# Output projection and first dense layer of a fused attention and MoE block: multiplied into one weight, and its stage dropped

## The chip, the cores and the metric

The kernel runs on 1 core of one Trainium2 chip. The metric is device time in microseconds (us) of one execution. A core has engines with queues of their own: TensorE (PE; its weight loads are listed as PEld), VectorE (DVE), ScalarE (ACT), GpSimd (POOL), and SyncE (SP), which issues the DMAs. They wait for one another by semaphores. TensorE multiplies a stationary 128x128 tile with a moving tile of up to 512 columns into one of eight PSUM banks.

## The reference

All in fp32, for x of 2 batches x 1024 tokens x 256 features:

```
q, k, v = x @ Wq.T + bq, ...            # 16 heads of 16
a   = sparse_attention(q, k, v)         # each query attends to 32 listed keys (or a dense form, by u_prev)
o   = a @ Wo.T + bo                     # output projection, 256 -> 256
h   = relu(o @ w1 + b1)                 # first dense layer, 256 -> 1024
x1  = x + h @ w2 + b2                   # 1024 -> 256
g   = gelu(x1 @ fc1.T + f1b)            # 256 -> 1024
c   = concat(g @ fc2.T + fc2_b, g @ experts[index].T + experts_b[index])   # 1024 -> 192 + 64
out = x1 + top-2-of-8 gated experts of c (router, 8 products 256 -> 256)
```

There is nothing between the projection and the first dense layer, so that h = relu(a @ (Wo.T @ w1) + (bo @ w1 + b1)).

## The kernel before

**Two paths.** The data decide at run time between a path for few distinct keys (`Few`, at most 256 of them; this is the one that runs with these inputs) and one for all keys (`Attention`). Both end in the same dense stage.

**Attention (Few).** An opening spreads the index lists, counts keys, and projects q, k, v on TensorE. Then `due()` lists the work in order of a time t, and each engine's function walks this one list and emits its own part. There are 64 "guard" jobs (8 units of 8), one at each t: TensorE forms guard scores of 128 queries against 256 keys for four heads, in two PSUM banks (lines 504 and 506; a job may only begin when VectorE has taken the maxima of the job two before it), and VectorE takes the maxima (line 737). 12 steps later (`LAG`) comes "score" job n = t - 12: TensorE, 2 products of 512 queries (line 524), ScalarE's exponential into `Pr` (line 657), VectorE's weighing (line 744). In between stand query transposes ("query_rows", line 489, copied by ScalarE at 649), key transposes ("score_keys", "guard_keys"), values products (line 540), and per unit "take", "norm" and "turn", which bring the result into `attT`. The banks of `psM` are handed out in turn over one list, `misc_order`: a user waits until the last but one has been copied out. `attention_done` is set by the copy of the last turn.

**Exact products.** Products of the dense stage are made of tiles rounded to a faster fp32 form (fp32r), each split into a rounded part hi (ScalarE or VectorE cast) and a rest lo (VectorE or GpSimd subtraction): `mm3` issues lo x hi, hi x lo, hi x hi, three products of 128x512 (lines 1544 to 1546). A plain fp32 product instead is run by the chip as two instructions.

**Weights.** `pieces` lists the weights in pieces of 128x1024 (fp32): early Wo (half a piece), w1 in two, w2 in two; late fc1 in two, WcA, WcB0, WcB1 (second layer of the second block), ew in four. SP loads piece i into slot i % 2 of `staged`, once the piece two before it is split (`load_pieces`, lines 1459 to 1472); ScalarE casts hi (`split_hi`, line 1478), GpSimd or VectorE subtracts lo (`split_lo`, line 1484). Early pieces are split during attention: ScalarE at guard jobs 4, 12, 20, 28 and 36, GpSimd at 6, 14, 22, 30 and 38. Late pieces are split in dense jobs named by `LATE_AT`; those with an even index by GpSimd, with an odd one by VectorE.

**Dense stage.** Four chunks of 512 tokens (`CHUNKS`). `dense_jobs` writes the order of jobs out: for a chunk, "h" (8 jobs of 6 products), "y" (2 jobs of 24), "gelu" (8 of 6), "c" (2 of 24), and for the chunk before, "router" and "experts" between them. The output projection is stage "ao", 2 jobs of 6 products per chunk: chunk 0's first of all, chunk 1's one before gelu 0 of chunk 0 and one behind gelu 7, those of chunks 2 and 3 between gelu and c of the chunk before. Its input is the attention output split in two (`attention_hi` on ScalarE, `attention_lo` on GpSimd, into tile `cT`), and its output `aoT` is evacuated by ScalarE (+ bias) into one of three buffers `V` and split by VectorE. All engines walk the jobs in this order. `AHEAD_AT` puts the first four jobs (ao 0, ao 1, h 0, h 1) between the last steps of attention on TensorE and ScalarE; of these, VectorE splits the two ao jobs ahead too, since the tile of h lies over memory that attention still uses.

**For the change** note: the first 12 guard jobs run with no score work beside them; `Pr` holds the exponentials from score 0 on and is free at tiles 2 to 5 before; `cols` holds the bias columns (bo 2, b1 8, b2 2, f1b 8).

## Time and profile before

| | |
|---|---|
| median of 3 runs | 569.64 us (569.31 to 569.93) |
| profiled execution | 570.82 us |
| its span in the trace | 568.4 us |
| TensorE busy | 521.5 us (92%) |
| VectorE busy | 408.6 us (72%) |
| ScalarE busy | 225.7 us (40%) |
| GpSimd busy | 84.2 us (15%) |

The trace is of one execution, some 2.4 us shorter than that execution's own time, since the span runs from the first to the last recorded instruction. Matmuls are pipelined: an instruction's listed time overlaps that of the next, so their cost in a row is the distance of their starts. "Granted clock" is the share of TensorE's full 2.4 GHz; 0.50 is 1.2 GHz. The opening runs to 56.41 us, guard jobs alone to 78.11, attention to about 271.3, and the dense stage to the end.

### The profile page before, as it was taken

To read this page: it belongs to the slowest core of one execution; us is meant where nothing else is said; L and a number is where in the kernel's file an instruction comes from. 1 tells how busy PE (TensorE), PEld (TensorE's weight loads), DVE (VectorE), ACT (ScalarE), POOL (GpSimd) and SP (SyncE) were. 2 spreads that over 40 slices of the span, in tenths; PEclk is the share of its full clock that TensorE was granted. 3 is DMA by queue.
4 is the path that set the end of the run, shared out by engine and by line. 5 is a ranking of instruction groups with operands and counts; after the bars stand their busy time and mean duration, and the time that the engine had idled before them with its cause. 6 is when DMAs were issued, how large, how long until landed. Compare 5 with 4: busy or idle time off the path is not lost.

```text
span 568.4 us, 7403 instructions
## 1 busy us (share of the span) xinstructions
PE 521.5 (92%) x2649; PEld 360.3 (63%) x2649; DVE 408.6 (72%) x788; ACT 225.7 (40%) x381; POOL 84.2 (15%) x94
## 2 busy tenths in 40 slices
PE   3897888999899999889969999999999999999896
PEld 1454445454454445436748887888878888788775
DVE  4887879878887777845867598483884839847295
ACT  4204476667665656764526240042400415003100
POOL 3002544315133120300141000010000100000000
PEclk9999699999999999999999999999999999999999
DMA  7200011101010000000451000100001000010000
GB/s 250 57 2 0 1 37 38 37 2 38 1 39 1 1 0 2 1 1 0 114 146 38 1 1 20 46 10 0 2 18 47 11 2 0 20 46 2 9 12 31
DMA packets 11756, 15.37 MB, mean 27 GB/s; under 512 B 5954, under 2 KB 8258, under 8 KB 11714
## 3 DMA queue, kind: packets, MB, share of 16 engines
q1 hardware_dynamic: 11714, 14.83, 8.5%
q8 instruction: 24, 0.39, 0.3%
q14 instruction: 18, 0.15, 0.1%
HBM read 12.73 MB, written 2.10 MB: 26 GB/s over the span
## 4 chain that ended last, share of the span: by engine, by line
PE 39%; DVE 6%; POOL 2%; issue 1%; DMA 1%; ACT 1%; SPq 0%; DVEq 0%; POOLq 0%
PE psG L1546 4%; PE psG L1545 4%; PE psG L1544 4%; PE psM L1544 3%; PE psM L1545 3%; PE psM L1546 3%; PE psS L1544 3%; PE psS L1545 3%; PE psS L1546 3%; PE psO L1544 3%; PE psO L1546 3%; PE psO L1545 3%; DVE hT_lo L1694 1%; DVE hT_hi L1692 1%; DMA staged<-ew_dram 1%
## 5 line engine op out<-in xcount | busy, mean ns | idle before, releaser
L737 DVE TENSOR_REDUCE few_Qa<-psG 128x2 fp32r<-128x512 f32 x116 | 74.7, 686 | 28.5 <-PE psG L506 28.4
L657 ACT ACTIVATE Pr<-psS 128x512 f32<-128x512 f32 x128 | 71.4, 599 | 28.5 <-PE psS L528 19.5
L744 DVE SCALAR_TENSOR_TENSOR Pr<-Pr,few_W 128x1024 f32<-128x1024 f32 x48 | 72.8, 1520 | 10.2 <-ACT Pr L657 10.1
L524 PE MATMUL psS<-few_QAT,few_KP 128*128 128x512 f32 x128 | 52.9, 457 | 10.5 <-ACT Pr L657 9.8
L504 PE MATMUL psG<-few_KG,QG 128*128 128x512 f32 x116 | 53.0, 515 | 2.9 <-DVE few_Qa L737 2.9
L1655 ACT ACTIVATE V<-psS,cols 128x512 f32<-128x512 f32 x16 | 11.0, 690 | 103.3 <-PE psS L1546 102.6
L1694 DVE TENSOR_TENSOR hT_lo<-V,hT_hi 128x512 fp32r<-128x512 f32 x64 | 46.5, 726 | 2.2
L506 PE MATMUL psG<-Mneg,few_identb 128*128 128x512 bf16 x116 | 46.8, 403 | 0.0
L524 PEld LDWEIGHTS psS<-few_QAT,few_KP 128*128 128x128 f32 x128 | 22.3, 188 | 38.2 <-issue 30.7
L1692 DVE CAST hT_hi<-V 128x512 fp32r<-128x512 f32 x64 | 34.2, 535 | 12.7 <-ACT V L1655 6.2
L540 PE MATMUL psO<-Pr,few_VA 128*17 128x512 f32 x256 | 33.5, 598 | 0.0
L1668 POOL TENSOR_TENSOR cT_lo<-attT,cT_hi 128x1024 fp32r<-128x1024 f32 x4 | 9.6, 2391 | 143.8 <-ACT cT_hi L1631 143.8
L706 DVE TENSOR_SCALAR few_EQ<-few_idxb,cst 128x1024 f16<-128x1024 f16 x64 | 28.8, 504 | 2.5 <-ACT few_idxb L588 2.5
L506 PEld LDWEIGHTS psG<-Mneg,few_identb 128*128 128x128 bf16 x116 | 11.4, 98 | 30.0 <-issue 29.8
L649 ACT CAST few_QAT<-psM 128x512 fp32r<-128x512 f32 x32 | 18.9, 590 | 21.0 <-PE psM L489 21.0
L504 PEld LDWEIGHTS psG<-few_KG,QG 128*128 128x128 f32 x116 | 23.4, 201 | 5.7 <-issue 4.2
L1692 DVE CAST cT_hi<-V 128x512 fp32r<-128x512 f32 x8 | 3.4, 427 | 32.7 <-ACT V L1660 32.7
L1544 PE MATMUL psO<-ew_lo,cT_hi 128*128 128x512 f32 x64 | 26.2, 410 | 0.4 <-DVE y L1806 0.4
L1544 PE MATMUL psM<-ew_lo,cT_hi 128*128 128x512 f32 x64 | 26.0, 406 | 0.2 <-DVE y L1806 0.2
L1546 PE MATMUL psO<-ew_hi,cT_hi 128*128 128x512 f32 x64 | 25.5, 398 | 0.0
L1545 PE MATMUL psO<-ew_hi,cT_lo 128*128 128x512 f32 x64 | 25.4, 397 | 0.0
L1545 PE MATMUL psM<-ew_hi,cT_lo 128*128 128x512 f32 x64 | 25.1, 392 | 0.0
(251 smaller groups left out, 1194.7 us busy)
## 6 DMA issues: line engine op xcount, KB each, us to landing
Pr<-xT_dram SPq DMA_DIRECT2D x2, 1024.0 KB, 8.6
staged<-w_dram SPq DMA_DIRECT2D x4, 512.0 KB, 3.7
x1T<-xT_dram SPq DMA_DIRECT2D x4, 512.0 KB, 4.2
staged<-ew_dram SPq DMA_DIRECT2D x4, 512.0 KB, 4.0
out_dram<-y SPq DMA_DIRECT2D x16, 128.0 KB, 1.7
staged<-fc_dram SPq DMA_DIRECT2D x2, 512.0 KB, 3.8
Pr<-wqkv_dram SPq DMA_DIRECT2D x1, 768.0 KB, 4.9
staged<-fc2a_dram SPq DMA_DIRECT2D x1, 512.0 KB, 3.4
```

What stands on the lines that cost most here:

```text
L504: nc.tensor.matmul(o, QG[:, (u // 2) % 2, st * P:st * P + P], self.KG[:, u % 2, 2 * p:2 * p + 2, :], start=True, stop=False)
L506: mm = nc.tensor.matmul(o, self.identb[:, :], Mneg[:, None, st * FEW_KEYS:(st + 1) * FEW_KEYS].to_broadcast([P, 2, FEW_KEYS]), start=False ...
L524: mm = nc.tensor.matmul(psS[:, f, :], self.KP[:, u % 2, j, r * P:r * P + P], self.QAT[:, u % 2, j // 2, q], start=True, stop=not logged)
L540: mm = nc.tensor.matmul(psO[VW * j:VW * j + VC, part, :], self.VA[:, b, r, h * VC:h * VC + VC], Pr[:, HG * r + j, 512 * part:512 * part + ...
L657: nc.scalar.activation(Pr[:, i % JOBS, 512 * f:512 * f + 512], psS[:, f, :], ACT.Exp, scale=SCALE).then_inc(self.s["s_exp"], 1)
L737: nc.vector.tensor_reduce(self.Qa[:, f % SLOTS, st, 2 * p:2 * p + 2, 48], self.guard_bank(i)[0][:, p, :].rearrange("p (h t) -> p h t", h=2 ...
L744: nc.vector.scalar_tensor_tensor(pr, pr, FMAX, self.W[:, r, :], ALU.min, ALU.mult).then_inc(self.s["s_prob"], 1)
L1544: nc.tensor.matmul(ps, w[0], a[1], start=start, stop=False)
L1545: nc.tensor.matmul(ps, w[1], a[0], start=False, stop=False)
L1546: return nc.tensor.matmul(ps, w[0], a[0], start=False, stop=stop)
L1692: link(nc.vector.tensor_copy(tile.hi[at], v))
L1694: nc.vector.tensor_tensor(tile.lo[at], v, tile.hi[at].bitcast(F32), ALU.subtract).then_inc(d["parts"], 1)
```

## The change

The two weights are multiplied once, Wo.T @ w1, on TensorE in plain fp32, and the joint bias b1 + bo @ w1 too. `Wo` and `w1` are loaded whole (w1 into both slots of `staged`), five "fuse" steps are listed at t = 0, 1, 3, 5 and 7 of `due()`, each behind the guard job of that t on TensorE: steps 0 to 3 make a quarter of the product each, step 4 the bias. ScalarE copies a quarter to `Pr` (tiles 2 to 5) and casts it to `w1.hi`; GpSimd makes `w1.lo`. ScalarE's first exponential waits for the four quarters. The stage "ao" is gone from the jobs, h reads the split attention output (now tile `aT`, one buffer for all chunks, refilled behind the chunk's last h job), and the jobs ahead of `attention_done` are h 0, h 1, h 2. Early pieces are now the two halves of w2, loaded behind step 4 and split in the places where w1's halves were (guard jobs 12/14 and 20/22). Late pieces have indices lower by three, so the engine that makes their lo changes.

```diff
+FUSED = 5
-AHEAD_AT = (1, 1, 4, 6)
+AHEAD_AT = (1, 2, 4)
+FUSED_AT = (0, 1, 3, 5, 7)
@@ due(), behind guard and the other entries of t
+                    for j in range(FUSED):
+                        if t == FUSED_AT[j]:
+                            yield "fuse", j
@@ misc_order()
+                    if what == "fuse":
+                        order.append(("fuse_out", i))
@@ Few.pool
-                    if what == "guard" and i % JOBS == 6 and i // JOBS < len(EARLY):
-                        split_lo(nc.gpsimd, pool, EARLY[i // JOBS:i // JOBS + 1])
+                    if what == "guard" and i % JOBS == 6 and 1 <= i // JOBS <= len(EARLY):
+                        split_lo(nc.gpsimd, pool, EARLY[i // JOBS - 1:i // JOBS])
+                    if what == "fuse" and i < FUSED - 1:
+                        fuse_lo(pool, i)
@@ Few.tensor
+                    if what == "fuse":
+                        fuse_tensor(pe, i, misc("fuse_out", i))
@@ Few.act
+                    if what == "fuse":
+                        fuse_act(act, i, self.misc_bank("fuse_out", i))
...
                     if what == "score":
                         if i == 0:
                             act.wait_ge(self.s["log_lo"], 1)
+                            act.wait_ge(d["fused"], FUSED - 1)
@@ pieces
-        early.append(("Wo", flat(Wo, 0, 512), [("WoT", 0, 512)]))
-        for name, w in (("w1", w1), ("w2", w2)):
-            for h in range(2):
-                early.append((name, flat(w, h * 1024, 1024), [(name, h * 1024, 1024)]))
+        for h in range(2):
+            early.append(("w2", flat(w2, h * 1024, 1024), [("w2", h * 1024, 1024)]))
@@ load_pieces
-                if i >= 2:
+                if i < 2:
+                    sp.wait_ge(d["fuse_full"], FUSED)
+                else:
                     sp.wait_ge(LD[f"w_lo{i % 2}"], i // 2)
@@ new
+        def load_fused(sp):
+            sp.dma_start(Wo[:, :, :], io["Wo"]).then_inc(LD["ld_wo"], 16)
+            sp.dma_start(staged[:, :, :], io["w1"]).then_inc(LD["ld_w1"], 16)
+        def fuse_tensor(pe, i, ps):
+            if i == 0:
+                pe.wait_ge(LD["ld_wo"], 16)
+                pe.wait_ge(LD["ld_w1"], 16)
+            if i < FUSED - 1:
+                rows_, _, cols_ = fused_part(i)
+                for o in range(KD):
+                    mm = nc.tensor.matmul(ps, Wo[:, o, rows_], staged[:, o, cols_], start=(o == 0), stop=(o == KD - 1))
+            else:
+                pe.wait_ge(L["cols"], 16)
+                nc.tensor.matmul(ps[:, 0:KW], ident, b1_in, start=True, stop=False)
+                for k in range(KW):
+                    for o in range(KD):
+                        mm = nc.tensor.matmul(ps[:, k:k + 1], staged[:, o, k * P:k * P + P], bo[:, o:o + 1],
+                                              start=False, stop=(k == KW - 1 and o == KD - 1))
+            mm.then_inc(d["fuse_full"], 1)
+        def fuse_act(act, i, ps):
+            act.wait_ge(d["fuse_full"], i + 1)
+            if i < FUSED - 1:
+                whole = Pr[:, 2 + i, 0:512]
+                nc.scalar.copy(whole, ps).then_inc(d["fuse_out"], 1)
+                act.wait_ge(d["fuse_out"], i + 1)
+                nc.scalar.copy(w1.hi[fused_part(i)[1]], whole).then_inc(d["fuse_hi"], 1)
+            else:
+                nc.scalar.copy(b1[:, :], ps[:, 0:KW]).then_inc(d["fuse_out"], 1)
+        def fuse_lo(pool, i):
+            pool.wait_ge(d["fuse_hi"], i + 1)
+            w = fused_part(i)[1]
+            nc.gpsimd.tensor_tensor(w1.lo[w], Pr[:, 2 + i, 0:512], w1.hi[w].bitcast(F32), ALU.subtract).then_inc(d["fused"], 1)
@@ dense_jobs
-            yield from jobs_of("ao", 0, range(KD), "act")
...
-                if c == 0:
-                    yield from jobs_of("ao", 1, range(1), "act")
...
-                    if c + 1 < CHUNKS:
-                        yield from jobs_of("ao", c + 1, range(c == 0, KD), "act")
@@ dense_tensor
-                if stage == "ao":
-                    weights("Wo")
+                if stage == "h":
+                    if n == 0:
+                        pe.wait_ge(d["fused"], FUSED - 1)
                     pe.wait_ge(d["at_lo"], c + 1)
...
-        LATE_AT = (("h", 2), ("h", 3), ("h", 5), ("h", 6), ("y", 0), ("y", 0), ("gelu", 1), ("gelu", 4), ("c", 0))
+        LATE_AT = (("h", 3), ("h", 4), ("h", 5), ("h", 6), ("y", 0), ("y", 0), ("gelu", 1), ("gelu", 4), ("c", 0))
@@ attention_hi
-            if c >= 2:
-                act.wait_ge(d["v_full"], number["experts", c - 2, TT * 5 - 1] + 1)
-            nc.scalar.copy(cT.hi[:, :, :], attT[:, :, c * QC:(c + 1) * QC]).then_inc(d["at_hi"], 1)
+            if c:
+                act.wait_ge(d["a_full"], number["h", c - 1, KW - 1] + 1)
+            nc.scalar.copy(aT.hi[:, :, :], attT[:, :, c * QC:(c + 1) * QC]).then_inc(d["at_hi"], 1)
@@ dense_vector
-                    if stage == "ao":
-                        if c and i == 0:
-                            dve.wait_ge(d["a_full"], number["h", c - 1, KW - 1] + 1)
-                        split(aoT, v, at)
```

## Rows read from the trace of the kernel before

**Rows 1.** The page's chain of work that ended last, shares by engine.

```profile
PE 39%; DVE 6%; POOL 2%; issue 1%; DMA 1%; ACT 1%; SPq 0%; DVEq 0%; POOLq 0%
```

**Rows 2.** Busy us (x instructions) by stretch: PE, PEld, DVE, ACT, POOL; clock, DMA, GB/s.

```profile
60.00:64.00 4.00, 2.43 (x6) 1.00 (x5) 4.00 (x6) 2.88 (x4) 0.90 (x1) 0.50 0.00 0
68.00:72.00 4.00, 3.96 (x21) 2.16 (x19) 3.40 (x7) 1.78 (x4) 4.00 (x9) 0.99 0.00 0
...
360.00:380.00 20.00, 20.00 (x90) 16.53 (x90) 14.05 (x24) 5.25 (x8) 2.43 (x1) 1.00 0.02 7
```

**Rows 3.** Timeline, TensorE, first guard job to first score: start us, us, instruction.

```profile
56.41 0.77 PE L504 MATMUL psG<-few_KG,QG 128*128 128x512 f32 x1
...
68.39 0.58 PE L504 MATMUL psS<-few_KG,QG 128*128 128x512 f32 x1
...
69.32 0.58 PE L504 MATMUL psG<-few_KG,QG 128*128 128x512 f32 x1
...
69.97 0.60 PE L489 MATMUL psM<-cst,few_Qa 128*128 128x128 f32 x4
70.33 0.47 PE L504 MATMUL psS<-few_KG,QG 128*128 128x512 f32 x1
...
76.64 1.04 PE L572 MATMUL psM<-cst,Qn 128*128 128x128 f32 x8
...
78.11 0.71 PE L524 MATMUL psS<-few_QAT,few_KP 128*128 128x512 f32 x2
```

**Rows 4.** Timeline, VectorE: the first guard job's maxima.

```profile
61.01 1.28 DVE L737 TENSOR_REDUCE few_Qa<-psG 128x2 fp32r<-128x512 f32 x2
```

**Rows 5.** Timeline, TensorE: plain fp32 products of the projections.

```profile
45.92 1.89 PE L432 MATMUL psM<-Pr 128*128 128x256 f32 x8
```

**Rows 6.** Router products after a gap (timeline), and two stretches with their clock.

```profile
537.20 0.25 PE L1606 MATMUL psM<-rw,cT_hi 128*128 128x16 f32 x1 [2.06 <-DVE cT_lo L1694]
537.30 0.25 PE L1607 MATMUL psM<-rw,cT_lo 128*128 128x8 f32 x1
...
284.00:288.00 4.00, 0.91 (x4) 0.43 (x4) 3.00 (x4) 1.82 (x3) 2.34 (x1) 1.00 0.64 139
...
539.20:543.20 4.00, 4.00 (x13) 3.20 (x12) 3.55 (x29) 0.23 (x1) 0.00 (x0) 0.58 0.01 2
```

**Rows 7.** Timeline: guard jobs 24, 40 and 56; a weight split and VectorE beside it.

```profile
113.23 0.40 PE L504 MATMUL psG<-few_KG,QG 128*128 128x512 f32 x1
...
163.66 0.39 PE L504 MATMUL psG<-few_KG,QG 128*128 128x512 f32 x1
...
213.04 0.40 PE L504 MATMUL psG<-few_KG,QG 128*128 128x512 f32 x1
...
133.00 2.38 POOL L1484 TENSOR_TENSOR w_lo<-staged,w_hi 128x1024 fp32r<-128x1024 f32 x1
...
133.29 3.18 DVE L744 SCALAR_TENSOR_TENSOR Pr<-Pr,few_W 128x1024 f32<-128x1024 f32 x1
```

**Rows 8.** Timeline, TensorE: the last turn of attention.

```profile
269.47 1.03 PE L561 MATMUL psM<-cst,few_An 128*128 128x128 f32 x8
```

**Rows 9.** Timeline, hand-over to the dense stage: GpSimd, ScalarE, VectorE, TensorE.

```profile
276.42 2.39 POOL L1484 TENSOR_TENSOR fc_lo<-staged,fc_hi 128x1024 fp32r<-128x1024 f32 x1 [43.56 <-ACT fc_hi L1478]
...
283.27 1.05 ACT L1478 CAST WcB_hi<-staged 128x1024 fp32r<-128x1024 f32 x1 [2.00 <-DMA staged<-experts_dram]
...
296.89 0.69 DVE L1694 TENSOR_TENSOR x_lo<-x1T,x_hi 128x512 fp32r<-128x512 f32 x1
...
296.72 0.68 PE L1544 MATMUL psS<-cT_lo,Wo_hi 128*128 128x512 f32 x1 [2.51 <-POOL cT_lo L1668]
...
299.33 0.63 PE L1544 MATMUL psS<-x_lo,fc_hi 128*128 128x512 f32 x1
```

**Rows 10.** Timeline, TensorE, chunk 1: first product of ao, first of c.

```profile
380.89 0.39 PE L1544 MATMUL psS<-cT_lo,Wo_hi 128*128 128x512 f32 x1
...
383.61 0.39 PE L1544 MATMUL psG<-hT_lo,WcA_hi 128*128 128x512 f32 x1
```

More of the change, by code:

```diff
@@ L400, in misc @@
                     if n >= 2:
-                        pe.wait_ge(self.s[order[n - 2][0]], order[n - 2][1] + 1)
+                        before, k = order[n - 2]
+                        pe.wait_ge((d if before == "fuse_out" else self.s)[before], k + 1)
                     return self.misc_bank(name, i)
@@ L724, in vector @@
                 for what, i in self.due():
-                    if what == "ahead" and i < KD:
-                        if i == 0:
-                            dve.wait_ge(self.s["q_lo"], FILLS)
-                        dense_vector(dve, jobs[i:i + 1], i)
                     if what == "guard":
@@ L1537, in bass_adaln_ffn @@
         for stage, c, i, e, n in jobs:
-            if stage in ("ao", "h", "y", "gelu", "c"):
+            if stage in ("h", "y", "gelu", "c"):
                 split_no[stage, c, i] = len(split_no) + 1
@@ L1569, in dense_tensor @@
                 cols_ = slice(i * P, i * P + P)
[L1570 to L1571 removed]
+                if stage == "h":
+                    if n == 0:
+                        pe.wait_ge(d["fused"], FUSED - 1)
                     pe.wait_ge(d["at_lo"], c + 1)
                     for k in range(KD):
[L1574 to L1579 removed]
+                        mm = mm3(ps, parts(w1, ALL, k, cols_), parts(aT, ALL, k, ALL), k == 0, k == KD - 1)
                 if stage == "y":
@@ L1834, in loads @@
                 if not att.dense:
+                    load_fused(sp)
                     load_pieces(sp, EARLY, eid)
@@ L1874, in work @@
                     attention_lo(pool, 0)
+                    for i in range(FUSED - 1):
+                        fuse_lo(pool, i)
                     split_lo(nc.gpsimd, pool, EARLY)
@@ L1886, in work @@
                 if att.dense:
+                    for i in range(FUSED):
+                        if i >= 2:
+                            pe.wait_ge(d["fuse_out"], i - 1)
+                        fuse_tensor(pe, i, psM[:, i % 2, :])
                     dense_tensor(pe, jobs[0:len(AHEAD_AT)])
@@ L1899, in work @@
                     attention_hi(act, 0)
+                    for i in range(FUSED):
+                        fuse_act(act, i, psM[:, i % 2, :])
                     split_hi(act, EARLY)
@@ L1913, in work @@
                 dve.wait_ge(s["attention_done"], 1)
-                if att.dense:
-                    for i in range(KD):
-                        dense_vector(dve, jobs[i:i + 1], i)
                 dve.wait_ge(L["cols"], 16)
-                dense_vector(dve, jobs[KD:], KD)
+                dense_vector(dve, jobs, 0)
             either(dve, work)
```

43 lines of the change are left out of this document (20 added, 23 removed).

## Prediction

> **What bounds the kernel now.** I read the page's chain of waits first: of the work that ended last, TensorE holds by far the largest share, VectorE the next [rows 1]. Since shares average stages with different limits, I went on to busy time by stretch. In the dense stage TensorE is busy 20.00 of 20 us [rows 2], at 2.4 GHz: each product taken out is worth its own spacing. In the opening, 60 to 64 us, it is busy 2.43 of 4 us at a granted clock of 0.50 (1.2 GHz), while VectorE is busy throughout; from 68 us on the clock is back and TensorE is busy 3.96 of 4 [rows 2]. Third came the timelines of the three stretches that the change touches: the opening from the first guard job (56.41) to the first score (78.11) [rows 3], the attention tail [rows 8], and the hand-over to the dense stage, where weights pass through a two-slot staging buffer [rows 9].
>
> **Dense products removed.** In steady chunks the two "ao" jobs of the next chunk (12 products) stand between 380.89 and the first product of "c" at 383.61: 2.72 us with no gap [rows 10]. Chunks 2 and 3 give 2 x 2.72 = 5.44 us. Chunk 1's second job (6 products) is worth half: 1.36. What would be late next is "c" waiting for VectorE's last gelu split, but that comes eight weight tiles into "c", 7 x 0.68 = 4.8 us after it starts, and one evacuation and one split are under 2 us: hidden. If VectorE had more backlog than that, it would cost the excess. Sum: -6.8.
>
> **Attention tail.** Twelve products (ao 0) between last score and values become h0 and h1, the same twelve; h1 no longer stands between norm and the last turn, and h0's wait on VectorE's ao split goes. The turn began at 269.47 [rows 8], while its input was ready about 0.3 us earlier: -0.5 at most, and it reaches only the start of the hand-over, so I book it there.
>
> **Hand-over.** Before, the first gelu product is at 299.33: ao 1's first job waited 2.51 us for the attention split, and ran with the start of gelu 0 at the low clock, 0.43 apart, not 0.23 [rows 9]. I do not book this wait as won, because something else is late: VectorE's last x1 split ended at 297.58 [rows 9]. The early weight pieces fall from five to two, so the parity of every late piece flips: fc1's first half, WcA and WcB1 go to GpSimd (2.39 each [rows 9]; VectorE takes half of that), and the first half of ew goes to VectorE, in front of y0's evacuation. A GpSimd split also stretches whatever VectorE starts beside it: 1.2 us became 3.18 [rows 7]. One leg of the staging chain is split, refill and landing: GpSimd's fc split ended at 278.81, the next tile was cast from 283.27, 4.46 us [rows 9]. ScalarE casts in job order, so each leg delays the evacuation queued behind it. Walking the chain from an attention end 0.5 earlier: WcA landed at about 280.4, WcB0 284.3, h7's split done 287.6 (as before), WcB1 288.3, ew0 290.5, its split on VectorE until 292.7, y0 and y1 evacuated and split by 297.4. So gelu 0 starts 1.9 us earlier, having stood idle longer; it starts at the low clock, and I charge 1.9 for that against 0.5 paid before. Together with the tail: -0.4. Bounds: if the clock holds and no split is stretched, -3; if each GpSimd split delays VectorE in full once more, +2.
>
> **Weight splits removed from the attention stage.** w1's and w2's four halves are cast and split in guard jobs 12/14, 20/22, 28/30 and 36/38; after, only two remain, in the first two places. Sixteen guard jobs with two splits took 113.23 to 163.66, 50.43 us; the next sixteen, without, 163.66 to 213.04, 49.38 [rows 7]. So a split costs 0.52: -1.05. Ends: 0 and twice that.
> The Trainium skill has a rule on this (page "SBUF — State Buffer", section "SBUF: two separate sides"): of a VectorE and a GpSimd instruction that both want the shared port pair, the later one blocks for the other's whole length. The trace agrees for the single instruction (3.18 beside a split of 2.38 us [rows 7]). Taken as the price of the stage it would give 2 x 2.4 = 4.8 us and a net gain of some 5 us; the two spans of sixteen jobs say that most of the block is absorbed, and I go by them.
>
> **Products added in the opening.** Five steps enter TensorE's queue behind guard jobs 0, 1, 3, 5 and 7.
> - Four steps of two plain fp32 products, 128x512. A plain fp32 product is two instructions: the projections run 8 instructions of 256 columns in 1.89 us with the overlapped end, 0.21 apart [rows 5], so 512 columns are 0.43 and a step of four is 1.72 at 2.4 GHz, 3.4 at 1.2 GHz.
> - One bias step: 17 fp32 products of one or eight columns, 34 instructions. The nearest row is the router, whose short products, each with its own 128x128 weights, stand 0.10 to 0.11 apart [rows 6]: 34 x 0.11 = 3.8. Upper end, had each weight load to finish alone (0.19): 6.5. Lower end 34 x 0.05 = 1.7, half the router's spacing.
> The skill has a lower figure (page "TensorE: Matmul & The Clock Gate", section "Back-to-back issue gap"): some 25 ns for a product of up to 64 columns. By that the step would be 0.9 us and the net gain 3 us larger. The router's spacing, four times as long, speaks against it.
>
> What hides them? Before, VectorE paces only the start: it is in the logarithms until 61.01, when it takes the first guard maxima [rows 4], and TensorE, two jobs ahead, waits 1.6 us. After 68 us TensorE has no gap. So I add up TensorE's queue from 56.41: guard 0 at the low clock 1.8; step 0 at the low clock 3.4; by then 5 us of unbroken work lie behind it, and I let the clock rise there (before, it rose after 6 us of it, the gap at 60.3 in between). Then eleven guard jobs at 0.93 (68.39 to 69.32 is one) = 10.2; three steps 5.2; bias 3.8; four groups of query transposes at 0.36 (69.97 to 70.33) and the score keys, 1.8; the next keys 76.64 to 78.11, 1.5 [rows 3]. Sum 27.7 against 21.70 before: +6.0. VectorE's twelve jobs (1.2 each, 61.01 to 75.4) lie under this; ScalarE's five copies and four casts (some 5 us) and GpSimd's four splits (5.1) too: before step 0's copy stands only ScalarE's cast of the logarithms, GpSimd's fourth split should end near 76, and the first score's new wait for it costs nothing. SP's loads (1.25 MB, issued at 20 us) are long there. The w2 loads now wait for the bias step, and still land before guard job 12's cast; late by more, they would hold ScalarE in front of its exponentials. The 6.0 passes on whole, since score 0 opens the pipeline of guards and scores. Ends: 4.5 (the clock rises 1.7 earlier, bias at its lower end) and 8.7 (bias at its upper end).
>
> **The clock behind the bias step.** At 537 us, 2.06 us of idling and then the router's short products preceded a fall to 1.2 GHz (0.58 over the next 4 us), whereas between 284 and 288 us, 0.91 us busy, the clock stayed at 1.00 [rows 6]. So 3.8 us of yet shorter products may bring a fall; it would cost 1.7 us if it lasts as behind 296.72, where the spacing was back at 2.4 GHz by 300.2 [rows 9]. I take +1.2, between 0 and 3.4.
>
> **Sum.** -6.8 - 0.4 - 1.05 + 6.0 + 1.2 = -1.05. The profiled execution took 570.82 (span 568.4 and 2.4 around it), 1.2 above the median; it becomes 569.77, and the median 569.64 becomes **568.6**.
>
> **Rivals.** A measurement of this kernel tells about 0.2%, 1.1 us, from no change.
> - Forecast, 567.4 to 569.8: chance 0.50; 0.20 of it is faster by over 0.2%.
> - The clock holds behind the bias step, and the hand-over begins warm: -1.05 - 1.2 - 1.0 = -3.3, 566.3. For it: the rise at 68 us was lasting. Against: [rows 6]. Chance 0.22.
> - The opening hides the new products after all, since guards wait for VectorE: +1 in place of +7.2, 562.4. For it: TensorE's gap at 60 us. Against: none after 68. Chance 0.05.
> - Slower: the bias step. Its short products run at 0.19 (+2.7) or are followed by two low-clock stretches (+2.2), all on TensorE's queue before score 0: net +1.2 to +3.8, 570.8 to 573.4. It decides from 2.2 us beyond my 7.2. For it: weights this large for one column. Against: the router's spacing. Chance 0.17.
> - The hand-over: y0's evacuation behind ew's split, and fc1 on GpSimd, put gelu 0 later than 299.33 by 2: net +1.4, 571.0. Chance 0.06.
>
> **Numbers.** Faster 0.22 + 0.05 + 0.20 of the forecast = 0.47; slower 0.17 + 0.06 = 0.23; within 0.2% the rest of the forecast, 0.30. The range leaves out the far rival and the outer part of the bias case: 565.4 to 571.8.
>
> **What would show it.** First score near 85 to 86 instead of 78.1, with TensorE unbroken from 56.4; bias instructions 0.11 apart; granted clock in the 4 us behind them; sixteen-job spans near 49.4; gelu 0 near 297.4; chunks of 68.9, not 71.6. Wrong would be: a first score before 81, or short products slower than 0.15.

## The result

The changed kernel takes 572.18 us (median of 15, 570.72 to 577.11), the kernel before 569.75 beside it (568.32 to 570.97): ratio 1.0053 [1.0035, 1.0070]. The forecast was 568.6 with a range to 571.8. The change made the kernel 0.5% slower.

### The profile page after: what moved, and what is told of

Its sections match the earlier page's. It is cut to its first block, busy times and chain, and to the rows that moved or that the text cites. A ratio compares the mean times of both kernels' runs of the same rounds, so it can differ in the third digit from the quotient of the medians.

```text
span 569.6 us, 7366 instructions
## 1 busy us (share of the span) xinstructions
PE 524.8 (92%) x2651; PEld 359.3 (63%) x2651; DVE 394.3 (69%) x771; ACT 223.0 (39%) x379; POOL 85.6 (15%) x96
## 4 chain that ended last, share of the span: by engine, by line
PE 75%; DVE 14%; ACT 6%; issue 2%; DMA 1%; SPq 0%; ACTq 0%; DVEq 0%
PE psS L538 7%; PE psO L554 6%; PE psG L518 4%; PE psG L520 4%; PE psM L1596 4%; PE psO L1596 3%; PE psM L1598 3%; PE psM L1597 3%; PE psG L1596 3%; PE psG L1597 3%; PE psG L1598 3%; PE psO L1598 3%; PE psO L1597 3%; PE psS L1596 3%; PE psS L1598 3%; PE psS L1597 3%
## 5 line engine op out<-in xcount | busy, mean ns | idle before, releaser
L757 DVE SCALAR_TENSOR_TENSOR Pr<-Pr,few_W 128x1024 f32<-128x1024 f32 x48 | 68.6, 1432 | 10.2 <-ACT Pr L674 10.1
L538 PEld LDWEIGHTS psS<-few_QAT,few_KP 128*128 128x128 f32 x128 | 22.3, 188 | 37.2 <-issue 29.7
L1703 ACT ACTIVATE V<-psG,cols 128x512 f32<-128x512 f32 x16 | 11.0, 690 | 48.7 <-PE psG L1598 48.7
L1716 POOL TENSOR_TENSOR aT_lo<-attT,aT_hi 128x1024 fp32r<-128x1024 f32 x4 | 9.7, 2432 | 132.6 <-ACT aT_hi L1679 132.6
L1597 PE MATMUL psM<-ew_hi,cT_lo 128*128 128x512 f32 x64 | 25.3, 395 | 0.0
```

The source lines that it names most:

```text
L538: mm = nc.tensor.matmul(psS[:, f, :], self.KP[:, u % 2, j, r * P:r * P + P], self.QAT[:, u % 2, j // 2, q], start=True, stop=not logged)
L757: nc.vector.scalar_tensor_tensor(pr, pr, FMAX, self.W[:, r, :], ALU.min, ALU.mult).then_inc(self.s["s_prob"], 1)
L1597: nc.tensor.matmul(ps, w[1], a[0], start=False, stop=False)
```

## The profile after

Profiled execution 571.68 us, span 569.6. The chain of work that ended last, shares by engine; it answers to [rows 1] and is again mostly TensorE (before, the chain could be followed back over half of the span only, so the shares themselves don't compare).

```profile
PE 75%; DVE 14%; ACT 6%; issue 2%; DMA 1%; SPq 0%; ACTq 0%; DVEq 0%
```

Busy time by stretch, the columns of [rows 2]: TensorE has no idle left at 60 us and has its clock there; it loses it between 76 and 80; the steady stage is as full as before.

```profile
60.00:64.00 4.00, 4.00 (x16) 1.66 (x14) 3.72 (x6) 3.17 (x4) 1.23 (x1) 1.00 0.01 4
...
76.00:80.00 4.00, 4.00 (x18) 2.79 (x17) 1.39 (x2) 1.40 (x5) 0.74 (x4) 0.57 0.55 168
...
360.00:380.00 20.00, 20.00 (x89) 16.32 (x88) 9.86 (x20) 2.16 (x3) 0.00 (x0) 1.00 0.12 39
```

Timeline of TensorE: guard job 0, the bias step (34 instructions, 72.65 to 76.36), the first score, guard jobs 24, 40 and 56, and the first product of c in chunks 1 and 2. They answer to [rows 3, 7, 10].

```profile
55.73 0.47 PE L518 MATMUL psG<-few_KG,QG 128*128 128x512 f32 x1
...
72.65 0.28 PE L1533 MATMUL psM<-cols,cst 128*128 128x8 f32 x2
72.79 3.71 PE L1536 MATMUL psM<-cols,staged 128*128 128x1 f32 x32
76.36 0.49 PE L492 MATMUL psM<-cst,few_Ka 128*128 128x128 f32 x2
...
84.52 0.71 PE L538 MATMUL psS<-few_QAT,few_KP 128*128 128x512 f32 x2
...
119.67 0.40 PE L518 MATMUL psG<-few_KG,QG 128*128 128x512 f32 x1
...
169.09 0.39 PE L518 MATMUL psG<-few_KG,QG 128*128 128x512 f32 x1
...
218.49 0.39 PE L518 MATMUL psG<-few_KG,QG 128*128 128x512 f32 x1
...
386.49 0.39 PE L1596 MATMUL psS<-hT_lo,WcA_hi 128*128 128x512 f32 x1
...
455.81 0.39 PE L1596 MATMUL psG<-hT_lo,WcA_hi 128*128 128x512 f32 x1
```

The hand-over (from the end of attention to gelu 0) in ScalarE's queue and VectorE's: the cast of WcA waits 4.02 us for its load, and the evacuation of h 6 (287.10) stands behind it; the next cast does the same to h 7 (291.22); ew's split stands in front of y0's evacuation (298.87).

```profile
286.15 1.05 ACT L1492 CAST WcA_hi<-staged 128x1024 fp32r<-128x1024 f32 x1 [4.02 <-DMA staged<-fc2a_dram]
287.10 0.68 ACT L1700 ACTIVATE V<-psS,b 128x512 f32<-128x512 f32 x1
290.26 1.05 ACT L1492 CAST WcB_hi<-staged 128x1024 fp32r<-128x1024 f32 x1 [2.48 <-DMA staged<-experts_dram]
291.22 0.68 ACT L1700 ACTIVATE V<-psS,b 128x512 f32<-128x512 f32 x1
...
297.73 1.23 DVE L1498 TENSOR_TENSOR ew_lo<-staged,ew_hi 128x1024 fp32r<-128x1024 f32 x1 [3.80 <-ACT ew_hi L1492]
298.87 0.75 DVE L1779 SCALAR_TENSOR_TENSOR x1T<-psO,cols,x1T 128x512 f32<-128x512 f32 x1
```

The same stretch on TensorE: three waits, of 2.60, 2.03 and 2.12 us, and the clock by stretch.

```profile
290.70 0.50 PE L1596 MATMUL psO<-hT_lo,w_hi 128*128 128x512 f32 x1 [2.60 <-DVE hT_lo L1742]
...
293.69 0.80 PE L1596 MATMUL psO<-hT_lo,w_hi 128*128 128x512 f32 x1 [2.03 <-DVE hT_lo L1742]
...
304.53 0.47 PE L1596 MATMUL psG<-x_lo,fc_hi 128*128 128x512 f32 x1 [2.12 <-DVE x_lo L1742]
```

```profile
288.00:292.00 4.00, 1.06 (x4) 0.49 (x3) 3.27 (x3) 1.64 (x2) 1.64 (x1) 0.95 0.52 119
292.00:296.00 4.00, 2.31 (x6) 1.83 (x7) 1.86 (x5) 1.04 (x1) 0.84 (x1) 0.50 0.83 213
...
304.00:308.00 4.00, 3.47 (x10) 2.81 (x11) 0.81 (x2) 0.69 (x1) 0.00 (x0) 0.66 0.00 0
```

Landmarks of the two traces (us), and how far the changed kernel is behind at each:

| | before | after | behind |
|---|---|---|---|
| guard job 0 | 56.41 | 55.73 | -0.68 |
| first score | 78.11 | 84.52 | +6.41 |
| guard job 24 | 113.23 | 119.67 | +6.44 |
| guard job 40 | 163.66 | 169.09 | +5.43 |
| guard job 56 | 213.04 | 218.49 | +5.45 |
| last copy to attT starts (end of attention) | 270.25 | 275.50 | +5.25 |
| gelu 0, chunk 0 | 299.33 | 304.53 | +5.20 |
| c 0 of chunk 0 | 312.03 | 317.12 | +5.09 |
| c 0 of chunk 1 | 383.61 | 386.49 | +2.88 |
| c 0 of chunk 2 | 455.23 | 455.81 | +0.58 |
| c 0 of chunk 3 | 524.10 | 525.13 | +1.03 |
| span | 568.4 | 569.6 | +1.2 |

The opening costs 7.09 and the attention stage gives 1.0, as forecast. What is missing is behind attention: the hand-over gives nothing, the chunks too little. And two profiled executions differ by 0.9 us where the medians differ by 2.4. Each execution's record has its span and mean granted clock; 2 x (1 - clock) x span is its time at 1.2 GHz. It is 15.9 to 22.7 us (median about 20) in the executions of the kernel before, and 21.6 to 36.8 (median 25) in the changed kernel's. Nine of the latter have at most 25.1 and a mean span of 569.4, six have 29.7 or more and 572.4: about 0.35 us of span per us at the low clock.

## Experiments

### Where the weights lie (e1, e2, e5)

The new tile b1 (32 bytes a partition) moves w1 and w2 from 64 bytes past a multiple of 256 to 96 past. e1 widens it to 64 bytes (128 past); e2 puts 32 unused bytes into the kernel before; e5 moves b1 behind the staging buffer, so that w1 is 64 past again.

```diff
 e1 -  b1 = sb("b1", [P, KW], F32)          +  b1 = sb("b1", [P, 16], F32)[:, 0:KW]
 e2 +  sb("shift32", [P, 8], F32)           (kernel before, ahead of w1)
 e5    b1 behind staged instead of ahead of w1
```

> The changed kernel with the new bias tile b1 made 64 bytes wide per partition instead of 32, so that w1, w2 and the staging buffer behind it start at a multiple of 64 bytes again. In the trace after, products with w1 or w2 as weights start 0.233 us apart, all others 0.227, and before all stood at 0.227. Theory A (the 32-byte shift of the weights slows each of them): spacing back to 0.227 for both, 96 x 0.006 = 0.6 us less per chunk, 2.2 to 2.5 us less in all than the changed kernel, ratio to the kernel before near 1.001. Theory B (the place of the moving tile aT): h stays at 0.233, time as in the changed kernel, ratio near 1.005.

> The kernel before with an unused tile of 32 bytes put in front of w1, nothing else changed. Theory A (32-byte shift): the spacing of h and y products goes from 0.227 to 0.233, time 2 to 2.5 us up, ratio near 1.004. Theory B: no difference, ratio 1.000.

> The changed kernel with the 32-byte tile b1 placed behind the staging buffer, so that w1 and w2 begin 32 bytes earlier, 64 bytes past a multiple of 256 as every weight did before; nothing else differs. Theory (the place of the weights costs 6 ns per 512-column product): the products of h and y in chunks 1 to 3 stand 0.227 apart instead of 0.233, a steady chunk takes 68.9 instead of 69.35 us, and the whole comes out 2.2 us under the changed kernel, a ratio of about 1.001. Rival (it is not the place but what the products work on, the sum of w1's making or of the new input tile aT): the spacing stays at 0.233 and the ratio at 1.005.

Measured: e1 572.07 (ratio 1.0049 [1.0035, 1.0063]), e2 571.94 (1.0044 [1.0031, 1.0057]), e5 573.96 (1.0081 [1.0068, 1.0093]). First and last of the 48 products of y in chunk 2 (chunks counted from 0), for the changed kernel, e2 and e5:

```profile
428.21 0.48 PE L1596 MATMUL psM<-hT_lo,w_hi 128*128 128x512 f32 x1
...
439.25 0.40 PE L1598 MATMUL psM<-hT_hi,w_hi 128*128 128x512 f32 x1
```

```profile
424.75 0.48 PE L1545 MATMUL psM<-hT_lo,w_hi 128*128 128x512 f32 x1
...
435.79 0.40 PE L1547 MATMUL psM<-hT_hi,w_hi 128*128 128x512 f32 x1
```

```profile
427.27 0.48 PE L1596 MATMUL psM<-hT_lo,w_hi 128*128 128x512 f32 x1
...
438.03 0.39 PE L1598 MATMUL psM<-hT_hi,w_hi 128*128 128x512 f32 x1
```

11.04 us in the changed kernel and in the old one shifted by 32 bytes, 10.76 with w1 back in its class (10.77 in the kernel before). Over all products with w1 or w2 as weights the spacing goes from 0.227 to 0.233; a chunk takes 72.03 instead of 71.6 in e2 and 68.89 instead of 69.34 in e5. That settles the mechanism: 0.45 us a chunk, by estimate 1.8 in all four. e1, 128 past, has 11.05 us and chunks of 69.35, so my theory A for it, that any multiple of 64 would do, was wrong. Shown is that 64 past a multiple of 256 is good and 96 and 128 past are not; the rule behind it is not. e5 as a whole is no better than the changed kernel, against my expectation; its median is 1.8 us higher. Five of its six executions spent 28 to 36 us at the low clock. In the profiled one (25.0 us) it is 1.68 ahead of the changed kernel at c 0 of chunk 3, and loses 1.3 of that behind the last router, where the clock is low for 6.8 us in place of 3.4: the span is 569.3 against 569.6. Why a shifted tile should go with more low clock I can't say; so the 0.45 a chunk is shown in the traces, and a gain in the time is not.

### Two chains in the opening (e3, e4, e11, e17)

e3 leaves the products bo @ w1 out of the bias. e4 leaves out all products of the five steps; ScalarE and GpSimd make w1.hi and w1.lo from w1 itself, at the same places. e17 is e5 with GpSimd's subtractions moved, e11 is e17 without the bias products.

```diff
 e3, TensorE
-  for k in range(KW): for o in range(KD): matmul(ps[:, k:k + 1], staged[:, o, ...], bo[:, o:o + 1], ...)
 e4, TensorE; ScalarE reads staged in place of ps
-  fuse_tensor(pe, i, misc("fuse_out", i))
 e11, e17, GpSimd
-  if what == "fuse" and i < FUSED - 1: fuse_lo(pool, i)
+  (split_keys 0, behind its instructions)  for j in range(FUSED - 1): fuse_lo(pool, j)
 e11, e17, ScalarE, ahead of score i
-  if i == 0: act.wait_ge(d["fused"], FUSED - 1)
+  if 2 <= i < FUSED + 1: act.wait_ge(d["fused"], i - 1)
```

> The changed kernel with the bias step cut to its first product: bo @ w1 is left out of the joint bias. The theory of the opening (TensorE's queue sets score 0): 32 instructions at 0.11 go, 3.5 us, and the fall of the clock behind them (76.4 to 79.8 us) too, 1.7 us: score 0 near 79.4 instead of 84.5, time 5 us below the changed kernel, near 567. Rival (the opening is paced by VectorE or GpSimd there): 1 us or less.

> The changed kernel without any product of the five steps: TensorE does nothing for them, ScalarE copies and casts w1 itself from the staging buffer (so the product with Wo and bo @ w1 are left out), all else as in the changed kernel. It shows the dense side of the change alone. By my sum: opening as before (-7.1 against the changed kernel), so 565 us, 5 us below the kernel before. If the low clock in the hand-over hung on the later opening only by chance of phase, the hand-over is as in the changed kernel: gelu 0 some 33 us behind the end of attention.

> As e5_align, without the products of the bias step (bo @ w1 is left out), and with GpSimd's four subtractions of w1.lo placed behind its splitting of the first unit's keys; only scores 2 to 5 wait for them. Theory (two chains of equal length end at the first score keys: TensorE's products, and GpSimd's queue, where 5 us of subtractions stand before the keys; leaving out the bias products alone moved nothing): with both shortened the first score comes at 80.5 to 82, against 85.4 with the bias products alone left out. Rival (a third cause, such as the clock after idling): not before 84.

> As e5_align, with GpSimd's four subtractions behind the first keys as in e11_no_bias_lo_late, but with the bias step left where the change put it. It is the fourth corner of a square: both chains long (score 0 at 84.4), the bias products out (85.4), both short (79.3). Theory (two chains of equal length): with GpSimd's alone shortened, TensorE's still ends at 84 to 85, ratio 1.004 to 1.008. Rival (GpSimd's queue alone held the opening, the bias step is cheap): score 0 at 80 to 82.

| | bias products | subtractions | first score | ratio |
|---|---|---|---|---|
| e5_align | in | ahead of the keys | 84.44 | 1.0081 |
| e3_nobias | out | ahead | 85.42 | 1.0027 [1.0012, 1.0042] |
| e4_nofuse | out, all products out | ahead | 84.94 | 1.0042 [1.0025, 1.0058] |
| e17_lo_late | in | behind | 86.19 | 1.0041 [1.0024, 1.0057] |
| e11_no_bias_lo_late | out | behind | 79.27 | 0.9946 [0.9925, 0.9966] |

Neither alone brings the first score nearer, both together bring it 5 us nearer or more: my expectations of e3 and e4, which knew of TensorE's queue alone, failed. e3 and e4 show the second chain, in GpSimd's queue: without the bias products TensorE idles 3.47 us for the keys (first row, e3), with no new product at all 6.36 (the others, e4).

```profile
75.99 0.69 PE L492 MATMUL psM<-cst,few_Ka 128*128 128x128 f32 x2 [3.47 <-POOL few_Ka L400]
...
66.79 1.28 POOL L1556 TENSOR_TENSOR w_lo<-Pr,w_hi 128x512 fp32r<-128x512 f32 x1
...
68.73 2.48 POOL L1556 TENSOR_TENSOR w_lo<-Pr,w_hi 128x512 fp32r<-128x512 f32 x2
...
73.71 1.25 POOL L1556 TENSOR_TENSOR w_lo<-Pr,w_hi 128x512 fp32r<-128x512 f32 x1
...
75.28 0.31 POOL L400 TENSOR_TENSOR few_Ka<-few_Kn,few_Ka 128x64 fp32r<-128x64 f32 x1
...
75.64 0.69 PE L492 MATMUL psM<-cst,few_Ka 128*128 128x128 f32 x2 [6.36 <-POOL few_Ka L400]
```

Before, the same key splits ran at 70.80 to 72.1; now 5 us of subtractions stand in front. The two chains end within 0.3 us of each other in the changed kernel (first keys split at 76.11, bias step over at 76.36). With either one left the clock falls too: in e3 and e4 while TensorE idles, in e17 near the end of the bias products, and in the profiles of e3 and e17 it stays low for 6.8 us in place of 3.4, which is why their first score is even later than e5's. In e11 it holds (busy time by stretch, e17, then e11).

```profile
76.00:80.00 4.00, 4.00 (x16) 2.98 (x17) 1.33 (x2) 0.90 (x3) 0.85 (x1) 0.50 0.40 105
```

```profile
76.00:80.00 4.00, 3.76 (x24) 2.49 (x22) 2.92 (x5) 2.42 (x7) 1.43 (x2) 1.00 0.33 133
```

The four product steps themselves are cheap: with them, and neither the bias nor the subtractions in the way, the first score is 1.2 us later than before the change (1.9 counted from guard job 0). TensorE has its clock from 60 us on there, where it was low to 68 before and to 64 in e8, which has no step in the opening; that this pays for the steps is argued, not measured by itself.

### The steps elsewhere (e7, e8)

```diff
 e7 +  yield "fuse", 0 ahead of "turn_counts", 0; yield "fuse", 1 ahead of "turn_counts", 1 (opening)
    -  FUSED_AT = (0, 1, 3, 5, 7)           +  FUSED_AT = (-99, -99, 1, 3, 15)
 e8 +  FUSED_AT = (13, 16, 24, 32, 40), quarters in a tile of their own
```

> As e5_align, with the five steps placed elsewhere: steps 0 and 1 in TensorE's two waits of the opening (before and behind the first turn of the counts, 1.1 and 1.4 us idle), 2 and 3 behind guard jobs 1 and 3, the bias step behind guard job 15, where TensorE idles 4 of 20 us; w2 is split 16 guard jobs later. Theory (the opening costs what TensorE's queue gets): first score at 80 to 82 instead of 84.5, the bias step costs 0 to 2 us behind it, whole 3 to 5 us under e5_align, ratio about 0.994. Rival (the steps disturb ScalarE and VectorE at the head of the opening, or the clock falls as before): first score not before 84, ratio as e5_align.

> As e5_align, with all five steps out of the opening: behind guard jobs 13, 16, 24, 32 and the bias at 40, each quarter held in a tile of its own instead of Pr; w2 is split at jobs 52 to 62. Theory (TensorE idles 2.8 us in each sixteen jobs of the steady stage and 4 just behind the first score, so a part of each step is hidden there): first score at 78.1 as before the change, half of the 10.7 us of products hidden, whole 1.5 to 3 us under e5_align. Rival (the stage is a chain through TensorE, whose idle time isn't free for others): last score where it was in the changed kernel, 264.3, or later; ratio 1.002 or more.

e7: 572.14, 1.0060 [1.0042, 1.0079], first score at 81.12 as expected, but guard job 24 at 119.71 as in e5 (119.59): the clock falls at 93.2, in the course of the bias step (90.4 to 94.9), and stays low to 100, which with the step itself took the gain back.

```profile
90.00:94.00 4.00, 4.00 (x33) 3.83 (x32) 2.53 (x4) 0.24 (x1) 0.00 (x0) 0.90 0.00 0
94.00:98.00 4.00, 4.00 (x14) 2.67 (x15) 0.62 (x1) 1.99 (x5) 0.00 (x0) 0.50 0.41 114
```

e8: 572.83, 1.0074 [1.0057, 1.0090]; the rival was right. The first score is at 77.22, but the sixteen jobs from guard 24 on take 51.6 us and the next 54.6, where 49.4 is the rule without steps: two steps of 1.7 us cost 2.2, and the bias step, with a stretch at the low clock (0.97 over the 54.6 us) and w2's splits, 5.2. TensorE's idle 6% there is hardly spare.

### The hand-over (e6, e9, e10)

e6 gives the late splits back to the engines that had them; e9 moves ScalarE's casts behind the evacuations of h; e10 does that to the kernel before.

```diff
 e6 -  VectorE splits late pieces k with k % 2 == 1
    +  VectorE splits late pieces k with (k - len(early)) % 2 == 0
 e9 -  LATE_AT = (h 3, h 4, h 5, h 6, y 0, y 0, gelu 1, gelu 4, c 0)
    +  LATE_AT = (h 3, h 4, y 0, y 0, gelu 1, gelu 3, gelu 5, c 0, c 1)
```

> As e5_align, and the late weight pieces are split by the engines that split them in the kernel before: fc1's first half, WcA, WcB1 by VectorE, the first half of ew by GpSimd. Theory (the flip of the engines stretches VectorE's splits of h and puts ew in front of y0's evacuation): TensorE's waits in y0, 2.6 and 2.0 us in the changed kernel, go to under 1 each, the low-clock stretch from 291 on starts later or goes, and the first gelu product comes 1.5 to 3 us earlier relative to the last score (40.2 us behind it in the changed kernel, 40.4 before). Rival (the staging chain's length decides, whoever splits): within 0.5 us of e5_align.

> As e5_align, with ScalarE's casts of the late weight pieces placed later: WcA and WcB0 behind the last h job (start of y) instead of behind h 5 and h 6, WcB1 and the four pieces of ew behind gelu 1, 3, 5 and c 0, 1. Theory (from the end of attention to the first gelu product it is 29.0 us in every kernel so far, 29.08 before the change and 29.03 after, since the evacuations of h 6 and h 7 stand in ScalarE's queue behind casts that wait for their DMA, so the products taken out there only turned into TensorE's waits, and these into low clock): TensorE's two waits in y0 go, the low-clock stretch from 291 too, and the distance falls from 29 to 22 to 25 us; the whole comes out 4 to 7 us under e5_align, ratio about 0.996. Rival (VectorE's splits, stretched by GpSimd's, hold the hand-over, not the casts): the distance stays within 1 us of 29.

> The kernel before, with the same later casts as e9_casts and nothing else. Theory: it gains 2 to 4 us in the same place (TensorE waited 3.09 there, and 2.5 at ao 1), and stands 1 to 3 us above e9_casts, since the products removed at the hand-over count once no chain of staging hides them. Rival (the casts are no limit before the change, where the ao products filled the wait): ratio 0.998 to 1.002.

| | end of attention to gelu 0 | median | ratio |
|---|---|---|---|
| before / after | 29.08 / 29.03 | | |
| e5_align | 28.82 | 573.96 | 1.0081 |
| e6_parity | 29.88 | 571.86 | 1.0044 [1.0030, 1.0057] |
| e9_casts | 25.33 | 568.71 | 0.9976 [0.9963, 0.9988] |
| e10_before_casts | 22.60 | 565.67 | 0.9927 [0.9914, 0.9940] |

e6 refutes the flip of the engines as a cause of the lost gain: TensorE's waits only change place (1.34 and 4.76 in y0), and gelu 0 is 1.1 us later than in e5. (Its median is 2.1 below e5's, but so is its time at the low clock, 26 us against 35.) e9 shows the casts: the evacuation is no longer behind a load, and gelu 0 is 3.5 us nearer.

```profile
286.85 0.69 ACT L1700 ACTIVATE V<-psS,b 128x512 f32<-128x512 f32 x1 [0.38 <-DVE hT_lo L1742]
...
288.67 1.05 ACT L1492 CAST WcA_hi<-staged 128x1024 fp32r<-128x1024 f32 x1 [1.14 <-DMA staged<-fc2a_dram]
...
293.30 0.51 PE L1596 MATMUL psO<-hT_lo,w_hi 128*128 128x512 f32 x1 [2.19 <-DVE hT_lo L1742]
...
303.43 0.47 PE L1596 MATMUL psG<-x_lo,fc_hi 128*128 128x512 f32 x1 [2.12 <-DVE x_lo L1742]
```

By the medians e9 gains 5.3 us on e5, within my expectation, but e5's is raised by its time at the low clock (35 us against 23); on the changed kernel it gains 3.5. The stretch of 25.3 us just misses the 22 to 25 expected, and 2.3 us are lost again behind c 0 of chunk 0, where the later casts bring two waits (0.57 and 0.97 us; 71.18 us to the next c 0, not 68.88). The kernel before gains 3.7 by the same edit (569.4 to 565.67), loses nothing behind c 0 (71.60 for 71.58), and keeps its lead of 0.5%: e10 was expected 1 to 3 us above e9 and is 3.0 below it. It has only one wait left in the stretch, of 0.76 us. Where e9 waits 2.12 ahead of gelu 0, for y1's evacuation and split, the kernel before has its ao job to run. Where e9 waits 2.19 in y0, VectorE's cast of h 7 is stretched, since GpSimd splits WcA beside it; in e10 VectorE does that split itself, behind h 7. So, by these rows, the flip of the engines, harmless in e6, does count once the casts are moved; that is not tested, as no run has both e9's casts and e6's engines. (e9's profiled execution is the slowest of its twelve, 572.73 us.) First two rows e9, third e10:

```profile
289.80 2.44 POOL L1498 TENSOR_TENSOR WcA_lo<-staged,WcA_hi 128x1024 fp32r<-128x1024 f32 x1 [4.66 <-ACT WcA_hi L1492]
289.93 2.59 DVE L1740 CAST hT_hi<-V 128x512 fp32r<-128x512 f32 x1
...
282.73 0.42 DVE L1692 CAST hT_hi<-V 128x512 fp32r<-128x512 f32 x1
```

### The clock (e13)

```diff
 e13, TensorE, ahead of the waits for k = 6 and 7 in y0, of gelu 0 (chunk 0) and of router 3 (the line of y0; the others alike)
+  for _ in range(8): nc.tensor.matmul(VBANK[2], w2.hi[:, 0, cols_], hT.hi[:, 0, :], start=True, stop=True)
```

> The changed kernel, with products whose result nobody reads in four waits of TensorE: eight each (1.8 us) before the last two products' waits in y0 (2.6 and 2.0 us idle), before gelu 0 of chunk 0 (2.1) and before the last router (2.1). Nothing else differs. Theory (a large part of what the change lost by the median is low clock behind these waits: 10.4 us of it in the hand-over, 3.4 to 6.8 behind the router, against 3.4 and 3.4 before the change): the clock stays at 1.00 from 291 to 309 and behind the router, each stretch of 3.4 us that goes is worth 1.7, the whole comes out 3 to 6 us under the changed kernel, ratio 0.995 to 1.000. Rival (the clock falls for another cause, or the waits grow by what the fillers take): low clock as before, ratio 1.005 or more.

572.58, ratio 1.0041 [1.0018, 1.0063]. The clock holds through y, where it had fallen to 0.50, and falls later:

```profile
292.00:296.00 4.00, 3.26 (x14) 2.35 (x13) 3.32 (x5) 1.64 (x2) 0.52 (x1) 1.00 0.64 142
296.00:300.00 4.00, 3.93 (x17) 2.89 (x16) 0.68 (x3) 1.72 (x2) 1.93 (x1) 1.00 0.48 140
...
304.00:308.00 4.00, 2.09 (x8) 1.38 (x8) 2.67 (x5) 0.00 (x0) 0.00 (x0) 0.94 0.32 112
```

But end of attention to gelu 0 is 28.44, only 0.6 us less, and the median does not move beyond its interval. TensorE is through with y at 302.9, and, with eight fillers in between, waits for VectorE: the evacuation of y0 stands behind ew's split, and the cast behind it is stretched to 1.86 us beside GpSimd's split of the attention output, so that y1's comes last.

```profile
300.42 1.23 DVE L1498 TENSOR_TENSOR ew_lo<-staged,ew_hi 128x1024 fp32r<-128x1024 f32 x1 [3.70 <-ACT ew_hi L1492]
301.56 0.75 DVE L1788 SCALAR_TENSOR_TENSOR x1T<-psO,cols,x1T 128x512 f32<-128x512 f32 x1
302.34 1.86 DVE L1749 CAST x_hi<-x1T 128x512 fp32r<-128x512 f32 x1
...
306.83 0.50 PE L1596 MATMUL psG<-x_lo,fc_hi 128*128 128x512 f32 x1 [1.91 <-DVE x_lo L1751]
```

While this chain sets the end of the stage, a faster TensorE in it is not worth much: the low clock there is mostly a symptom. My expectation of 3 to 6 us was wrong.

### Together (e12, e14, e15, e16)

```diff
 bias step in four parts (columns 2p and 2p + 1 each), FUSED = 8
 e12 +  FUSED_AT = (-99, -99, 1, 3, 13, 15, 17, 19), steps 0 and 1 as in e7, casts as in e9
 e14 +  FUSED_AT = (0, 1, 3, 5, 13, 15, 17, 19), subtractions as in e11, casts as in e9, fillers
 e15    e14 with LATE_AT = (h 3, h 7, y 0, gelu 0, 2, 4, 6, c 0, c 1)
 e16    e10 with the filler ahead of router 3
```

> e9_casts and e7_gaps together, and the bias step cut into four of 10 instructions, behind guard jobs 13, 15, 17 and 19, so that no run of short products is longer than 1.1 us. Theory: first score at 81, no low clock near 91 (it fell there behind the whole bias step in e7_gaps, for 6.8 us), distance of the hand-over as in e9_casts: another 3 to 5 us under e9_casts, ratio 0.988 to 0.992. Rival (short products in small lots let the clock fall all the same): a low-clock stretch between 88 and 105, and no more than 1 us under e9_casts.

> All that was found, together: b1 behind the staging buffer, the steps of the product behind guard jobs 0, 1, 3 and 5 with GpSimd's subtractions behind the first keys, the bias step in four parts behind guard jobs 13 to 19, the casts placed later (as e9_casts), and fillers as in e13_filled (one group of eight in y0 instead of two). Theory: first score at 79.3, parts of the bias hidden (as in e12_best1, 34.9 us from first score to guard job 24), the hand-over 22 to 24 us and without low clock, chunks of 68.9: 556 to 560 us, ratio 0.977 to 0.983. Rival (the gains overlap, each wait removed shows the next): not under 563.

> As e14_best2, with fc1's second half cast behind h 7 instead of h 4 and the pieces behind it one to two jobs later, so that VectorE has no weight split among its splits of h. Theory (the last wait of y0, 2.2 us in e12_best1, comes from VectorE's 1.2 us split of fc1 and from GpSimd's split of WcA beside the split of h 7): gelu 0 another 1 to 2 us earlier than in e14_best2. Rival (later pieces hold the first c product, which needs WcB1): c 0 later than in e14_best2 although gelu 0 is earlier.

> The kernel before with the later casts (as e10_before_casts) and the filler of eight products before the last router: what the kernel before gives with the same help as e14_best2. Theory: 1.7 to 3.4 us under e10_before_casts, near 563, ratio 0.989, so that the joined weights, placed well, are worth 4 to 6 us. Rival: they are worth nothing once both have the same staging, and e14_best2 is no faster than this.

| | first score | attention to gelu 0 | median | ratio |
|---|---|---|---|---|
| e12 | 80.99 | 25.36 | 565.66 | 0.9933 [0.9910, 0.9957] |
| e14 | 78.52 | 23.70 | 560.91 | 0.9860 [0.9837, 0.9882] |
| e15 | 79.56 | 22.95 | 561.32 | 0.9870 [0.9850, 0.9889] |
| e16 | 77.03 | 22.58 | 564.17 | 0.9909 [0.9894, 0.9924] |

In four parts the bias step is cheap: first score to guard job 24 takes 34.86 in e12 and 35.15 in the changed kernel, although its 4.4 us of products are in there; w2's two splits, 1.0 us, are not, so some 0.7 is what it costs. As a whole e12 is 3.1 us under e9, the lower end of what was expected. The clock holds (busy time by stretch, e12).

```profile
84.00:106.00 22.00, 21.98 (x129) 14.32 (x129) 17.34 (x21) 14.07 (x33) 5.57 (x9) 1.00 0.01 3
```

e14, below, has no low clock from 58 to 528 us and waits 0.22 us at gelu 0, behind its eight fillers. It is 1.4% faster than the kernel before, the fastest of all, though short of the 556 to 560 expected. e15 brings gelu 0 0.75 us nearer but a product of c 0 waits 1.32 for a split (0.58 in e14), as its rival said.

```profile
78.52 0.48 PE L540 MATMUL psS<-few_QAT,few_KP 128*128 128x512 f32 x1
...
293.95 0.50 PE L1600 MATMUL psG<-x_lo,fc_hi 128*128 128x512 f32 x1 [0.22 <-DVE x_lo L1755]
```

e16's filler gains 1.5 us on e10, a little less than the 1.7 to 3.4 expected. Against e16, the kernel before with the same casts and that filler, e14 is 3.3 us faster (560.91 to 564.17): that is what the joined weights are worth in the best placing found here. It is not all theirs to give: e14 has two more groups of fillers, and still loses 2.3 us behind c 0 of chunk 0 (71.18) that e16 doesn't. Of e14's 8.5 us over the kernel before, 5.2 are the staging order and the filler, which have nothing to do with the change.

## Why the prediction was wrong

**The opening: right number, by half of the reason.** +7.2 forecast, +7.09 measured. The terms held on TensorE: bias instructions 0.11 apart (3.71 us for 34, forecast 3.8), a fall of the clock behind them (0.57 from 76 to 80), steps of 1.7 (62.37 to 65.94 holds one and two guard jobs of 0.93; forecast 1.72). The Trainium skill's lower figure (page "TensorE: Matmul & The Clock Gate", section "Back-to-back issue gap") would have made the 34 together 0.9 us, as an estimate; that figure is for products by themselves, without their weight loads, and the trace, with a load for each, does not agree. Wrong was the sentence that ScalarE's casts and "GpSimd's four splits" lie under this: they are a second chain of the same length, since they stand in GpSimd's queue in front of the keys (e4, e11, e17). I had counted their time and when the last would end, not what queues behind them, though it ended where I said, near 76.

**Attention: right.** The sixteen jobs take 49.42 instead of 50.43, 1.01 for a forecast of 1.05.

**The hand-over: the step that failed most.** Forecast -0.4 there and -1.36 for ao 1's second job, together -1.76 (by the terms of the prediction, -1.9 and +1.4, it is -0.5 and not -0.4); measured -0.16 from the end of attention to c 0 of chunk 0. The failed step is "So gelu 0 starts 1.9 us earlier". The tail gave 0.2 of its 0.5. Of the chain, the first legs came as walked, counted from the end of attention: WcA's cast at 10.65 (forecast 10.65), h 7's split done at 18.1 (17.9), ew's split at 23.5 (22.9). Its last leg did not: y1 was to be split at 27.65, and gelu 0 starts at 29.03, where it did before (29.08). After the wait of 2.60 us the clock fell at 291.6, so that the last 27 products of y took 8.6 us and not 6.3. I had charged a fall from gelu 0 on only. With the clock held there (e13) VectorE's queue ends at nearly the same place, 28.44: y0's evacuation behind ew's split, and a stretched cast. The two limits lie so close that removing one gives 0.6. What TensorE no longer does became its waits, 6.75 us in three for 5.60 in two before, while ao 1's first job had run where TensorE now waits 2.12. The second job's 1.36 is gone too, and gelu 0 to c 0 takes 12.59 for 12.70: TensorE is at the low clock for 3.4 us there, a fall that I had charged. e9 and e10 show what the chain hangs on, by moving the late casts. The engines' flip, which I charged and which the rival of 0.06 rested on, does not decide where the change left the casts (e6); its other half, y0's evacuation behind ew's split, is what e13 waits for.

**Dense products: -6.8 was too much.** Beside the 1.36 just told, the two steady chunks with ao jobs gave 2.2 and 2.3, not 2.72, and the next, with nothing to give, took 0.45 longer (69.32 for 68.87): the placing of b1 costs 0.45 a chunk (e2, e5). No row of the kernel before could show it; I had costed the new tile at nothing without saying so.

**The clock: under-counted.** I charged one fall behind the bias step, 1.2 us. The profiled execution behaves like that, the median one has about 5 us more at the low clock than before; by the slope of 0.35 that is, as an estimate, some 1.2 to 1.8 us of the 2.4. In which stretch an execution loses it varies: the profiles of e3 and e9 have a low stretch of 6.8 us from 75 on where the changed kernel's has 3.4, and one more of 3.4 from 256 on. That more falls follow from the waits is argued, not shown; the fillers of e13 did not lower the median.

**Sum.** Forecast -1.05; +1.6 (hand-over), +1.4 (chunks) and +1.2 or so (clock in the median execution) give +3.1; measured +2.4, the difference being guard job 0, 0.68 earlier in this execution. The rival with the slower sign (bias step, 570.8 to 573.4) holds the time, but not by its mechanism as far as the profile shows: neither 0.19 per product nor a second low-clock stretch was there. The median execution has 3.5 us more at the low clock than the profiled one, and e3, e7, e9 and e17 show stretches of 6.8 in place of 3.4; whether it had the second stretch there is open.

## What to carry to other kernels

Where a stage ends by a chain of staged loads, products taken out of it buy little: measure the stage from its start to its end before and after, and first move what waits for a load out of the queue of what doesn't. Check work put on a side engine for what stands behind it in that engine's queue, not only for when it is over. When a new small tile goes in front of weights, compare the spacing of their products before and after. Cut a run of short products into parts between longer ones.

## What the runs showed of the hardware

- 32 bytes of shift of two weight tiles cost 6 ns of 227 on each 512-column product, in two different kernels (11.04 against 10.77 us for 48 products), with the moving tile where it was. The Trainium skill (page "SBUF — State Buffer", section "Operand start alignment") asks only for multiples of the element size, and says that its runs timed nothing; both places fulfil it.
- 34 short products in a row (3.7 us at 0.11 each) came with a fall of the clock: just behind them in the changed kernel, from 3.2 us on in e17 and from 2.9 us on in e7. Four lots of 10 between longer products did not (e12, e14, e15).
- Over the executions of the changed kernel each us more at the low clock went with 0.35 us more of span, not the half that a bound TensorE would give. That part of it falls in waits is my reading; e13, which holds the clock in such waits and gains nothing by the median, fits it.
- A cast of VectorE that started beside a GpSimd split of 2.4 us took 2.59 us, where it takes 0.42 alone (e9 against e10).
